# Attention context of each head computed token-major, without a copy and three transposes

## The reference

```
q, k  = x @ q_w[h], x @ k_w[h]                      # 384 x 128
v     = sum_e gate_v[:, h, e] * (x @ v_w[h, e])     # 384 x 128, 2 of 8 experts are not zero
att   = softmax(q @ k.T / sqrt(128))                # 384 x 384
ctx   = att @ v                                     # 384 x 128: the context
out  += sum_e (gate_o[:, h, e] * ctx) @ o_w[h, e]   # 384 x 1024
```

## Time and profile before

| | us |
|---|---|
| median of 3 runs | 823.56 (823.32 to 823.94) |
| the profiled execution, whole | 826.44 |
| its span, first to last instruction | 824.4 |
| TensorE busy in the span | 812.7 |
| VectorE, GpSimd, ScalarE busy | 489.0, 461.0, 376.4 |

### The profile page before, as it was taken

How to read it: one execution, slowest core, us unless ns; L and a number is a source line. 1 busy time by engine, 2 the same in 40 slices (tenths; PEclk the granted TensorE clock), 3 DMA queues, 4 the chain that set the end, 5 groups by cost and what they waited for, 6 DMA issues and landing times.

```text
span 824.4 us, 14155 instructions
## 1 busy us (share of the span) xinstructions
PE 812.7 (99%) x5016; PEld 650.6 (79%) x5016; DVE 489.0 (59%) x1112; ACT 376.4 (46%) x615; POOL 461.0 (56%) x296
## 2 busy tenths in 40 slices
PE   8999999999999999999999999999999999999998
PEld 7999998888888778898578578578578588588476
DVE  7999973444444155998554554655655545645645
ACT  5333335555665343334624634634634534535531
POOL 4577875343334434547664665565674665664652
PEclk9999999999999999999999999999999999999999
DMA  8666663442222328643598597597597597697684
GB/s 295 185 194 178 201 191 107 144 136 81 97 76 78 103 77 323 213 129 134 122 245 304 119 266 273 125 264 269 132 271 258 131 264 261 140 257 262 147 217 172
DMA packets 66177, 153.38 MB, mean 186 GB/s; under 512 B 9392, under 2 KB 22320, under 8 KB 66128
## 3 DMA queue, kind: packets, MB, share of 16 engines
q1 hardware_dynamic: 51472, 120.73, 42.7%
q0 software_dynamic: 10944, 24.82, 16.5%
q10 hardware_dynamic: 3712, 7.18, 3.2%
HBM read 122.06 MB, written 37.97 MB: 194 GB/s over the span
## 4 chain that ended last, share of the span: by engine, by line
PE 83%; POOL 4%; issue 4%; DMA 3%; DVE 3%; ACT 1%; SPq 0%; ACTq 0%; DVEq 0%; POOLq 0%
PE bank L1586 22%; PE bank L1588 21%; PE bank L1587 21%; PE bank L1917 12%; POOL mask_scratch L501 3%; PE bank L1640 2%; PE bank L1729 2%; PE bank L1633 2%; PE bank L1701 2%; DVE scratch L1004 1%; DMA w_raw<-in_units 1%; DMA mask_scratch<-scratch,cell 1%; POOL w_lo L497 1%; DMA mask<-mask_scratch 0%; ACT scratch L725 0%
## 5 line engine op out<-in xcount | busy, mean ns | idle before, releaser
L557 POOL TENSOR_TENSOR w_lo<-w_raw,w_hi 128x1024 fp32r<-128x1024 f32 x67 | 164.4, 2456 | 140.3 <-ACT w_hi L812 132.2
L1586 PE MATMUL bank<-w_hi,hT_hi 128*128 128x512 f32 x480 | 190.1, 396 | 1.9 <-POOL w_lo L548 1.2
L1588 PE MATMUL bank<-w_hi,hT_lo 128*128 128x512 f32 x480 | 187.5, 391 | 0.0
L1587 PE MATMUL bank<-w_lo,hT_hi 128*128 128x512 f32 x480 | 187.5, 391 | 0.0
L497 POOL TENSOR_TENSOR w_lo<-w_raw,w_hi 128x1024 fp32r<-128x1024 f32 x39 | 94.7, 2431 | 103.7 <-ACT w_hi L640 83.5
L812 ACT ACTIVATE w_hi<-w_raw 128x1024 fp32r<-128x1024 f32 x84 | 88.7, 1056 | 127.0 <-PE bank L1588 98.9
L1586 PE MATMUL bank<-hT_hi,w_hi 128*128 128x384 f32 x320 | 108.2, 338 | 1.2 <-POOL w_lo L497 1.2
L1586 PEld LDWEIGHTS bank<-w_hi,hT_hi 128*128 128x128 f32 x480 | 90.6, 189 | 21.7 <-POOL w_lo L548 1.7
L1588 PE MATMUL bank<-hT_hi,w_lo 128*128 128x384 f32 x320 | 107.1, 335 | 0.0
L1587 PE MATMUL bank<-hT_lo,w_hi 128*128 128x384 f32 x320 | 107.1, 335 | 0.0
L1588 PEld LDWEIGHTS bank<-w_hi,hT_lo 128*128 128x128 f32 x480 | 90.1, 188 | 19.1
(11 more groups left out here) (228 smaller groups left out, 1279.6 us busy)
## 6 DMA issues: line engine op xcount, KB each, us to landing
w_raw<-in_units SPq DMA_DIRECT2D x145, 512.0 KB, 3.9
late<-in_units SPq DMA_DIRECT2D x56, 512.0 KB, 7.7
scratch<-slots_scratch SPq DMA_DIRECT2D x7, 512.0 KB, 7.3
scratch<-in_src_row ACTq DMA_DIRECT2D x8, 384.0 KB, 4.3
scratch<-in_dst_row ACTq DMA_DIRECT2D x8, 384.0 KB, 6.3
sums_scratch<-zeros SPq DMA_DIRECT2D x1, 1536.0 KB, 8.3
sums_scratch<-x SPq DMA_DIRECT2D x1, 1536.0 KB, 11.3
x<-sums_scratch SPq DMA_DIRECT2D x3, 512.0 KB, 4.8
```

The source lines that it names most:

```text
L557: pool.tensor_tensor(w_lo[:, s, :], w_raw[:, s, :], w_hi[:, s, :].bitcast(fp32), ALU.subtract).then_inc(lo_ready[s], 1)
L1586: pe.matmul(dst, a_hi, b_hi, start=first, stop=False)
L1587: pe.matmul(dst, a_hi, b_lo, start=False, stop=False)
L1588: return pe.matmul(dst, a_lo, b_hi, start=False, stop=last)
```

## The change

`f_attend` now holds a 128 x 128 block of the turned probabilities still and moves the values, 128 columns. It writes one 128 x 128 block of the context for each token block t, with tokens on the partitions, into bank 0 (`CF = 0`) for every head. There are three token blocks and three key blocks m, each with the three matmuls of `three`. The copy on ScalarE, its buffer, the three transposes and the two semaphores between them go. VectorE waits for `f_context`, the end of `f_attend`, and reads bank 0. The wait for the copy ahead of value unit 0 goes too. The order of everything else stays.

```
 def f_attend(head):
     pe.wait_ge(fv_lo_done, head + 1)
-    for m in range(NT):
-        pe.wait_ge(f_pT_lo, head * NT + (NT if m == NT - 1 else 2))
-        last = three(bank[context_bank(head)][:, 0:N], v2_hi[:, m, :],
-                     v2_lo[:, m, :], pT_hi[:, m, :], pT_lo[:, m, :], m == 0, m == NT - 1)
+    for t in range(NT):
+        tok = slice(t * P, (t + 1) * P)
+        for m in range(NT):
+            if t == 0:
+                pe.wait_ge(f_pT_lo, head * NT + (NT if m == NT - 1 else 2))
+            last = three(bank[CF][:, tok], pT_hi[:, m, tok], pT_lo[:, m, tok], v2_hi[:, m, :],
+                         v2_lo[:, m, :], m == 0, m == NT - 1)
     last.then_inc(f_context, 1)
-
-def context_turns(h):
-    pe.wait_ge(context_ready, h + 1)
-    for t in range(NT):
-        last = turn(bank[turned_bank(h)][:, t * P:(t + 1) * P], context[:, t * P:(t + 1) * P])
-    last.then_inc(context_T, 1)
...
-            def context_of(head):
-                act.wait_ge(f_context, head + 1)
-                act.activation(context, bank[context_bank(head)][:, 0:N], ACT.Copy).then_inc(context_ready, 1)
...
             def gate_rows_of(h):
-                dve.wait_ge(context_T, h + 1)
+                dve.wait_ge(f_context, h + 1)
...
-                        dve.tensor_scalar(gated_rows[:, k, t, :], bank[turned_bank(h)][:, t * P:(t + 1) * P],
+                        dve.tensor_scalar(gated_rows[:, k, t, :], bank[CF][:, t * P:(t + 1) * P],
...
             def gate_context(e):
                 if e == 0:
-                    dve.wait_ge(context_T, FH)
+                    dve.wait_ge(f_context, FH)
...
-                    pe.wait_ge(context_ready, h)
...
-                    context_turns(0)
...
-                context_turns(h)
```

More of the change, by code:

```diff
@@ L92 @@
 VF = ((2, 3, 4), (0, 1, 2))
+CF = 0
 SF = TF = (5, 6, 7)
@@ L107, in k_bank @@
     return 1 if h == 1 else 7
[L110 to L115, removed]
 def act_rows(n):
@@ L222, in gnn_switch_kernel @@
         gated = scratch[:, 4224:4992].rearrange("p (b n) -> p b n", b=2)
-        context = scratch[:, 4992:4992 + N]
         v_sum = scratch[:, 5376:5376 + N].rearrange("p (t d) -> p t d", t=NT)
@@ L309, in gnn_switch_kernel @@
         slots_known, experts_known = sem("slots_known"), sem("experts_known")
-        context_T, gated_rows_ready = sem("context_T"), sem("gated_rows_ready")
+        gated_rows_ready = sem("gated_rows_ready")
         gated_rows_landed, slots_landed = sem("gated_rows_landed"), sem("slots_landed")
@@ L322, in gnn_switch_kernel @@
         f_probs_T, f_pT_hi, f_pT_lo = sem("f_probs_T"), sem("f_pT_hi"), sem("f_pT_lo")
-        f_context, context_ready = sem("f_context"), sem("context_ready")
+        f_context = sem("f_context")
         gated_ready, gc_hi_done, gc_lo_done, out_added = (sem("gated_ready"), sem("gc_hi_done"), sem("gc_lo_done"),
@@ L877, in _ @@
                 hi_ring("v", h, 2)
-                if h == 1:
-                    context_of(0)
                 hi_ring("v", h, 3)
@@ L905, in _ @@
                     y_out(h - 1, i, 0)
-                    if i == 3:
-                        context_of(h)
                     if h == FH - 1 and i == SLOTS - 2:
@@ L1545, in gate_context @@
                 dve.tensor_tensor(gated[:, e % 2, :].rearrange("p (t d) -> p t d", t=NT),
-                                  bank[turned_bank(FH - 1)][:, 0:N].rearrange("p (t d) -> p t d", t=NT),
+                                  bank[CF][:, 0:N].rearrange("p (t d) -> p t d", t=NT),
                                   gates[:, :, c:c + 1].to_broadcast([P, NT, P]), ALU.mult).then_inc(gated_ready, 1)
```

## The result

The changed kernel takes 833.41 us (median of 4 runs, 832.78 to 834.31), the kernel before 823.68 beside it (4 runs, 823.32 to 823.94): a ratio of 1.011, 95% interval 1.0095 to 1.0127, or 9.7 us more. Forecast were 832.4 us and 8.8 more, with an attend of 27 steps of 0.1115 us. The profiled execution took 834.31 with a span of 832.6.

What follows compares the result with a forecast made beforehand. TensorE's queue was taken to bound the kernel. New matmuls 24.08 us, less 12.69 for the old and 4.60 for the turns, plus 2.04 for round 7, gave +8.8: 832.4 us, range 829 to 858.

Steps and rivals of the forecast that it cites:

- TensorE's queue sets the end, and all counts one to one: From 362 to 786 us, each microsecond added to or taken from TensorE's queue moves the end by as much.
- s: Step of one 128-column matmul in the new attend, 0.1115 us, near range 0.108 to 0.118; 27 per head, eight heads.
- plain `float32` rival: In the new attend, a narrow float32r matmul costs as much as plain float32, 0.223 us a step: 856.5 us; chance 0.25.
- the one without overlap: In the new attend, weight load and stream don't overlap, 0.175 us a step: +22.6, 846.1 us; chance 0.05.
- the faster load: In the new attend, loads run faster in a stream, about 0.08 us a step: +2.0, 825.6 us; chance 0.04.
- The turns cost 0.61 us amid the rounds: Taking out the three transposes between rounds 4 and 5 saves 0.61 us for each of heads 1 to 7.
- Round 7 gives some back: In heads 1 to 6, round 7 waits for VectorE's eviction of round 5, losing 0.34 us each, 2.04 in all.
- the hand-over from VectorE to TensorE: Time from the end of VectorE's eviction of round 5 to the start of round 7, taken as 0.05 us.
- Head 7 has no stall: VectorE has one operation of 0.55 us there in place of 1.64, so round 7 doesn't wait in head 7.
- ScalarE's copy is worth nothing: Dropping ScalarE's copy of the context, 0.49 us eight times, saves nothing, as only the turns wait for it.

Runs made afterwards that it cites:

- the kernel with the early eviction: The changed kernel with VectorE's eviction of round 5 put ahead of the six gating operations for heads 1 to 6; 830.44 us, ratio to before 1.0067.

## Why the prediction was right, point by point

- **TensorE's queue sets the end, and all counts one to one.** Right. Between the attends of heads 1 and 7 six periods grew by 1.26 us each and one of them by 0.1 more, 7.7 us; from head 0 to head 1 it is 1.1 more; behind the attend of head 7 another 0.8. The sum is 9.6 us, and the runs differ by 9.7. The spans alone, 824.4 and 832.6, mislead by 1.4 us: so much earlier the attend of head 0 begins in the profiled execution after, in code that the change doesn't touch. In the one before, the clock had fallen in the first layer, and the forecast took its span and its 2.9 us over the runs' median without seeing this:

```profile
139.20:142.70 3.50, 3.50 (x12) 3.50 (x13) 0.00 (x0) 2.60 (x6) 3.50 (x13) 0.51 0.44 146
```

- **s = 0.1115 us, because a load of 128 x 128 can't hide behind 128 columns.** Right in size, 0.112, and in that the columns don't set it: the step is the same for 32 to 128 columns and 0.120 for 256. That it is the load fits all runs and is not isolated by one. The row that sized it, plain float32 with 128 columns, was a lucky choice: in the same trace a plain float32 record of 384 columns (line 1729, two groups of 64 columns of the array side by side) takes 0.323 us, so at 128 columns the stream alone explains its 0.111. The two loads 0.11 us apart were the evidence that held. The plain `float32` rival (0.223) and the one without overlap (0.175) fall, and so does the faster load; the sentence of the Trainium skill beside it (TensorE: Matmul & The Clock Gate, section Back-to-back issue gap: about 81 ns for a load and matmul of 128 columns) doesn't hold for `float32r` here, where 112 were measured.
- **The turns cost 0.61 us amid the rounds.** Right: 61.19 + 27 x 0.112 - 1.59 - 0.61 = 62.0 is the period of the kernel with the early eviction. The 0.28 us of it that is the broken run came back, 0.33, when the turns moved.
- **Round 7 gives some back.** Right in place, cause and number of heads, too small in size: 0.47 us in place of 0.34. The end of the eviction was exact, 5.43; the step that was off is the hand-over from VectorE to TensorE, sized 0.05 from a transpose that waits for one semaphore, measured 0.20 before an output round. That is 0.13 x 6 = 0.8 us, which covers what separates 8.8 from 9.6. A round waits for four semaphores one after the other; that this makes the hand-over longer is argued, not shown.
- **Head 7 has no stall, ScalarE's copy is worth nothing.** Right: six waits, not seven; ScalarE's 0.49 us eight times left no mark, since the periods close without it.
- **What the forecast left out** is the clock. It stayed at 0.999 to 1.000 with 128 columns, so nothing came of it. That was luck: nothing in the forecast said so, and with 64 columns every execution lost some of it.

## What to carry to other kernels

Turning a matmul so that the small side moves can save a transpose and still lose: count the matmuls, and price each by the longer of its stream and its weight load, here 0.112 us for a `float32r` block at 32 to 128 columns, 0.120 at 256. When work leaves a queue, look for what was hidden under it, here an eviction that ended 0.34 us before its round could start. And the order of work on the bounding engine is itself worth time: the same transposes and the same attend, put where they don't break a run of another kind of matmul, gave 3.8 us (0.5%) with nothing removed.

## What the runs showed of the hardware

A busy TensorE can lose its clock. Attends of 32, 64 and 96 moving columns, bound by weight loads, were followed by falls to 1.2 GHz in four, three and one places of the profiled execution, with TensorE having work throughout; each fall cost 1.7 us, or 1.2 where it hid the wait of round 7, and the kernel that computes less became slower than the one that computes all, 838.6 and 839.8 against 833.4 us. The Trainium skill (TensorE: Matmul & The Clock Gate, section HAM oscillation — how this bites in real kernels) ties such falls to idle gaps between bursts of matmuls; here there was none: with 32 columns the first fall came behind the attend of head 0, at 364.6 us, and TensorE's list of waits is empty from 311 us to there. The trace of the kernel before has a fall that fits it, at 139 us, behind waits of 0.33 and 1.36 us; the changed kernel has a wait of 1.33 us there and no fall.

Where a matmul stands has a price of its own. Three transposes cost 0.33 us beside `float32r` work and 0.61 between rounds of `float32` lanes. That it is the change of kind that costs is the reading, not shown by itself.
